# Four phases of a two-layer transformer kernel: engine loops written out as straight-line code

## The chip, the cores and the metric

One core of one Trainium2 chip runs the whole program. The metric is the device time of one execution in microseconds. Differences are judged against the median of several runs of the kernel before.

## The reference

Two layers work on x of shape 2 x 2048 x 256 (batch, token, channel). Each layer has an attention part and a feed-forward part, each behind a layer norm with a scale and shift from a small modulation product, and each added back with a gate.

```python
# layer 0
c_kv = h @ W_kv_down                      # 128 wide
k_rope, q_rope = rotary(c_kv @ W_k_rope), rotary(h @ W_q_rope)
k, v, q = heads(c_kv @ W_k_up), heads(c_kv @ W_v_up), heads(h @ W_q)
attn = softmax(causal((q k + q_rope k_rope) / scale)) v @ W_o
out  = top-2 experts of 8, three ReLU layers each
# layer 1
z   = softmax over tokens of (h @ W_A.T) / 4          # 16 heads
out[i] = sum over j <= i of z[i - j] * v[j]           # a Toeplitz product per head
out = out @ W_O.T + b_O
# last feed-forward: x_prev is x shifted by one token
r = sigmoid(mix_r(h, h_prev) @ W_r.T);  k = relu(mix_k(h, h_prev) @ W_k.T) ** 2
x = x + gate * r * (k @ W_v.T)
```

## The kernel before

The kernel is nine phases, one after the other, with a barrier between two phases: setup, project, attention, attn_out, route, experts, mix, mix_out, ffn. In each phase every engine has its own instruction stream, written by hand, and waits on semaphores. Nothing is scheduled by a planner.

Tokens go through the phases in chunks of 512 (`CH`), four chunks (`NCH`) for each of two batches (`NB`). A half-iteration is one chunk of one batch. Phases project, mix and ffn share the helper `one_ahead` (lines 236 to 244). It first starts the first half-iteration, then runs `work(it, 0, ...)` and `work(it, 1, ...)` for three values of `it` in an engine loop (`Fori`), and writes the fourth value out behind the loop. `work` also prepares the half-iteration that comes next. TensorE, VectorE and ScalarE each run this helper with their own `work`. In a loop, `it` is a register: addresses and semaphore values that depend on it are computed by small register instructions of that engine (FUSED_REGOPS, ALU_OP, MOVE), and the loop ends in a COMPARE_BRANCH.

What matters of the four stages:
- **project** (50 to 212 us). A half-iteration on TensorE is transposes of the normalised rows (L433), the products of `ckv`, `q`, rope, `k` (L467) and `v` (L486) into six PSUM banks. On VectorE it is the low halves of q (L358), the next layer norm (L72 to L81), two rope blocks (L364 to L373) and the low halves of k (L358). TensorE's `freed` makes it wait until VectorE has read a bank: the first product of `ckv` for batch 0 waits for the rope block of `kr` of the half before (L373), and `q0` of batch 1 does too. SyncE stores 11 pieces for each half (L327 to L336), in a loop of its own.
- **mix** (1817 to 1900 us): layer norm, transposes (L1633), z (L1641) and values (L1658), then a softmax over all tokens, written out.
- **Toeplitz products** (1900 to 2046 us, inside phase mix). For each head and batch SyncE loads a skewed copy of z of 1 MB into one of four buffers `tz` (L1560), TensorE makes 16 products with fp32 weights (L1673), and VectorE copies the result (L1598). Each of the three has a loop of eight iterations with four of these groups in its body.
- **ffn** (2112 to 2221 us). On TensorE a half-iteration is k products (L1905), the next transposes (L1895), r products (L1915) and v products (L1924). On VectorE it is the next normalise (L1823), the next mix (L1833, L1837) and the output (L1857, L1859). GpSimd squares k (L1798), SyncE stores (L1811), both in loops of four.

Attention (212 to 1225 us) has a loop too (`units`, L616; SyncE's at L729): one iteration is two units of one group of four heads and one batch. Its iteration is far longer than the others.

Of the kernel before, what the change touches and what calls it, by code (L numbers as in the profile page):

```python
# [21 lines left out]
NCH = T // CH  # L22
NT = T // P
NH, HD, DR, DC = 16, 16, 32, 128
# [211 lines left out]
def one_ahead(eng, start, work):  # L236


    start(0, 0)
    with eng.Fori(0, NCH - 1) as it:  # L240
        work(it, 0, (it, 1))
        work(it, 1, (it + 1, 0))
    work(NCH - 1, 0, (NCH - 1, 1))
    work(NCH - 1, 1, None)


def phase_project(nc, g):


    with ExitStack() as c:  # L250
# [62 lines left out]
        @block.sync  # L313
        def _(sp):
            for s in (*tr_done, *ht_ready, *stored, *ckv_ready, *rope_ready, *hi_ready, *lo_ready, *va_ready):
                sp.sem_inc(s, 1)
            for dst, src in ((wkv[:, :, :], g.i["wkv"].rearrange("(k p) n -> p k n", p=P)),
                             (wq[:, :, :], g.i["wq"].rearrange("(k p) n -> p k n", p=P)),
                             (wqr[:, :, :], g.i["wqr"].rearrange("(k p) n -> p k n", p=P)),
                             (wkr[:, :], g.i["wkr"]), (wku[:, :], g.i["wku"]), (wvu[:, :], g.i["wvu"])):  # L320
                sp.dma_start(dst, src).then_inc(w_ld, 16)
            sp.dma_start(cs[:, :], g.i["cs"]).then_inc(cs_ld, 16)
            with sp.Fori(0, NCH) as it:
                for b in range(NB):
                    cols = bass.ds(b * T + it * CH, CH)
                    sp.wait_ge(rope_ready[b], 2 * it + 3)
                    sp.dma_start(g.d_qrh[:, cols], roth[0:32, b, 0, :]).then_inc(stored[b], 16)  # L327
                    sp.dma_start(g.d_krh[:, cols], roth[0:32, b, 1, :]).then_inc(stored[b], 16)
                    sp.wait_ge(hi_ready[b], 4 * it + 5)
                    sp.wait_ge(lo_ready[b], 4 * it + 5)  # L330
                    for n, (dh, dl) in enumerate(((g.d_qh, g.d_ql), (g.d_kh, g.d_kl))):
                        for k in range(KT):
                            sp.dma_start(dh[k * P:(k + 1) * P, cols], hi[:, b, n, k, :]).then_inc(stored[b], 16)
                            sp.dma_start(dl[k * P:(k + 1) * P, cols], lo[:, b, n, k, :]).then_inc(stored[b], 16)
                    sp.wait_ge(va_ready[b], 2 * it + 3)
                    sp.dma_start(g.d_va[:, bass.ds(b * NT + it * TPC, TPC), :],  # L336
                                 va[:, b].rearrange("p t h d -> p t (h d)")).then_inc(stored[b], 16)
            for b in range(NB):
                sp.wait_ge(stored[b], 16 * NST * NCH + 1)
# [1160 lines left out]
def phase_mix(nc, g):  # L1500


    with ExitStack() as c:
# [37 lines left out]
        @block.sync  # L1541
        def _(sp):
            for s in (*mix_done[0], *mix_done[1], *tr_done, *ht_ready, *z_ready, *v_ready, *mix_read[0], *mix_read[1]):
                sp.sem_inc(s, 1)
            sp.dma_start(wa[:, :, :], g.i["wa"].rearrange("(k p) h -> p k h", p=P)).then_inc(w_ld, 16)
            sp.dma_start(wv[:, :, :], g.i["wv"].rearrange("(k p) n -> p k n", p=P)).then_inc(w_ld, 16)

            sp.wait_ge(zn_ready, 1 + NB)
            sp.dma_start(g.d_z[:, :, 0:P], zero[:, :, :]).then_inc(zstored, 16)
            sp.dma_start(g.d_z[:, :, P:], z[:, :, :]).then_inc(zstored, 16)  # L1550
            sp.wait_ge(zstored, 32)
            with sp.Fori(0, NH // 2) as it:
                for p in range(2):
                    for b in range(NB):
                        sp.wait_ge(mix_done[p][b], it + 1)


                        row = g.d_z[bass.ds(it * 2 + p, 1), b, 1:1 + T]
                        src = bass.AP(row.tensor, row.offset, [[1, P], [1, T]])
                        sp.dma_start(tz[:, p, b, :], src).then_inc(toep_ld[p][b], 16)  # L1560

        @block.vector
        def _(dve):
            ch = Chain(dve, chain_s)

            def normalise(it, b):
                ch.at((it * NB + b) * LN_LINKS)
                dve.wait_ge(tr_done[b], 2 * it + 1)
                ln_rows(dve, ch, g.x, b * NT + it * TPC, hn[:, b], ln, b, it).then_inc(hn_ready[b], 1)

            def work(it, b, ahead):
                if ahead:
                    normalise(*ahead)
                if not isinstance(it, int):
                    values(it, b)

            def values(it, b):
                for j in range(2):
                    dve.wait_ge(v_done[b], 2 * it + j + 1)
                    dve.tensor_copy(vn[:, bass.ds(b * NT + it * TPC + 2 * j, 2), :],  # L1580
                                    ps[:, 4 + 2 * b + j, :].rearrange("p (t c) -> p t c", t=2)).then_inc(v_ready[b], 1)
            one_ahead(dve, normalise, work)
            ch.at(NCH * NB * LN_LINKS)
            for b in range(NB):
                dve.wait_ge(z_ready[b], NCH + 1)
                ins = dve.tensor_reduce(nmax[:, b:b + 1], z[:, b, :], AX.X, ALU.max, negate=True)
                ins.then_inc(nmax_ready, 1)
            dve.wait_ge(exp_ready, NB)
            ch.link(dve.reciprocal(zrec[:, :], zsum[:, :]))
            for b in range(NB):  # L1590
                dve.tensor_scalar(z[:, b, :], z[:, b, :], zrec[:, b:b + 1], None, ALU.mult).then_inc(zn_ready, 1)
            for b in range(NB):
                values(NCH - 1, b)
            with dve.Fori(0, NH // 2) as it:
                for p in range(2):
                    for b in range(NB):
                        dve.wait_ge(mix_done[p][b], it + 2)
                        dve.tensor_copy(g.mixed[:, b * NT:(b + 1) * NT, bass.ds((it * 2 + p) * HD, HD)],  # L1598
                                        ps[:, 2 * p + b, 0:C].rearrange("p (t d) -> p t d", d=HD))\
                           .then_inc(mix_read[p][b], 1)  # L1600
# [26 lines left out]
        def _(pe):  # L1627
# [8 lines left out]
            def work(it, b, ahead):  # L1636
                pe.wait_ge(w_ld, 32)
                pe.wait_ge(ht_ready[b], 2 * it + 3)
                pe.wait_ge(z_ready[b], it + 1)
                for k in range(KT):  # L1640
                    ins = pe.matmul(ps[0:NH, 2 + b, :], wa[:, k, :], ht[:, b, k, :], start=(k == 0), stop=(k == KT - 1))  # L1641
                ins.then_inc(z_done[b], 1)
                if isinstance(it, int):

                    if ahead:
                        transposes(*ahead)
                else:
                    values(it, b, ahead)
# [15 lines left out]
            for b in range(NB):  # L1664
                pe.wait_ge(v_ready[b], 2 * NCH + 1)

            with pe.Fori(0, NH // 2) as it:
                for p in range(2):
                    for b in range(NB):
                        pe.wait_ge(toep_ld[p][b], (it + 1) * 16)  # L1670
                        pe.wait_ge(mix_read[p][b], it + 1)
                        for d in range(NT):
                            ins = pe.matmul(ps[:, 2 * p + b, d * HD:C], tz[:, p, b, d * P:(d + 1) * P],  # L1673
                                            vn[:, b * NT:(b + 1) * NT - d, bass.ds((it * 2 + p) * HD, HD)],
                                            start=(d == 0), stop=(d == NT - 1))
                        ins.then_inc(mix_done[p][b], 1)
# [76 lines left out]
def phase_ffn(nc, g):  # L1753

    with ExitStack() as c:
# [34 lines left out]
        @block.gpsimd  # L1790
        def _(pool):
            pool.memset(ht[:, :, :, CH:CH + 1], 0.0).then_inc(zero_done, 1)
            with pool.Fori(0, NCH) as it:
                for b in range(NB):
                    pool.wait_ge(v_done[b], 2 * it + 1)
                    for k in range(KT):
                        pool.wait_ge(kr_ready[b], 2 * it + k + 2)
                        pool.tensor_tensor(ka[:, b, k, :], kr[:, b, k, :], kr[:, b, k, :], ALU.mult)\  # L1798
                            .then_inc(ka_ready[b], 1)

        @block.sync
        def _(sp):
# [2 lines left out]
            sp.dma_start(wr[:, :, :], g.i["wr"].rearrange("(k p) n -> p k n", p=P)).then_inc(w_ld, 16)  # L1805
            sp.dma_start(wk[:, :, :], g.i["wk"].rearrange("(k p) n -> p k n", p=P)).then_inc(w_ld, 16)  # L1806
            sp.dma_start(mu[:, :, :], g.i["mu"]).then_inc(w_ld, 16)
            with sp.Fori(0, NCH) as it:
                for b in range(NB):
                    sp.wait_ge(y_ready[b], 2 * it + 3)  # L1810
                    sp.dma_start(g.out[bass.ds(b * T + it * CH, CH), :].rearrange("(t p) c -> p t c", p=P), y[:, b])\  # L1811
# [233 lines left out]
```

## Time and profile before

| | |
|---|---|
| median of 3 runs | 2202.44 us (2201.98 to 2204.1) |
| the profiled execution's own time | 2223.14 us |
| its span, first to last instruction | 2221.6 us |
| TensorE / VectorE / ScalarE / GpSimd busy | 77% / 55% / 39% / 13% |
| mean granted TensorE clock | 0.89 of full speed |

The profiled execution is 20.7 us longer than the median of the others, and 1.5 us of it lie outside the span. Stages are read from windows of the span. TensorE appears twice: PE is the matmul, PEld the load of its weights. A small q behind an engine's name marks its sequencer, which handles branches, register instructions and the issue of DMAs. These don't count as busy time.

### The profile page before, as it was taken

The page shows a single profiled execution, that of the slowest core. Times are in us where ns is not written, and L with a number is a line of the kernel's source. Part 1 is how long each engine was busy: PE and PEld are TensorE (multiplying, and loading weights), DVE is VectorE, ACT ScalarE, POOL GpSimd, SP SyncE. Part 2 cuts the span into 40 slices and gives each one's busy share as a digit, 9 for nine tenths or more (in the row PEclk, how much of TensorE's full clock was granted, in tenths as well). Part 3 has the DMA queues.
Part 4 walks back from the last instruction along what each step waited for, and adds up shares of the span by engine and source line. Part 5 has one row for each costly group of instructions (what it writes and reads, how often), then busy time and mean ns, then how long its engine had stood idle before and what let it go on. Part 6 is the DMA issues. An engine that isn't in the chain of part 4 may idle for free. (4 is left out here: it accounts for less than half of the span.)

```text
span 2221.6 us, 34675 instructions
## 1 busy us (share of the span) xinstructions
PE 1714.1 (77%) x12628; PEld 847.3 (38%) x12628; DVE 1214.5 (55%) x3101; ACT 860.1 (39%) x1137; POOL 287.6 (13%) x356
## 2 busy tenths in 40 slices
PE   4774278999999999999999264304888977999988
PEld 3332012333333333333333232102434454899556
DVE  4675577887877878697850134301444545101466
ACT  0231034566656666566667013202545513000133
POOL 1001283000000000000000110272212100000011
PEclk8898589999999999999999676656999969999989
DMA  5234941221203030303000310027666300774011
GB/s 177 93 117 147 164 137 62 57 40 49 49 26 72 25 72 22 65 25 73 25 25 36 113 61 0 32 107 159 131 141 144 100 5 0 234 235 140 1 38 47
DMA packets 88965, 180.41 MB, mean 81 GB/s; under 512 B 12529, under 2 KB 61330, under 8 KB 83538
## 3 DMA queue, kind: packets, MB, share of 16 engines
q1 hardware_dynamic: 69072, 109.73, 20.3%
q0 software_dynamic: 18656, 66.31, 8.8%
q8 instruction: 98, 1.61, 0.3%
q10 hardware_dynamic: 1090, 2.36, 0.3%
q14 instruction: 49, 0.40, 0.1%
HBM read 119.38 MB, written 57.85 MB: 80 GB/s over the span
## 5 line engine op out<-in xcount | busy, mean ns | idle before, releaser
L858 ACT ACTIVATE at_pr<-ps 128x1024 f32<-128x1024 f32 (+3 forms) x640 | 548.5, 894 | 361.9 <-PE ps L798 233.6
L892 DVE TENSOR_REDUCE at_mx<-ps 128x1 f32<-128x512 f32 x768 | 489.1, 685 | 173.2 <-PE ps L748 163.6
L795 PE MATMUL ps<-at_sq,at_sk 64*128 64x512 f16 (+3 forms) x2560 | 346.3, 349 | 22.7 <-DMA at_sq<-at_mr 18.7
L748 PE MATMUL ps<-at_sk,at_sq 64*128 64x512 f16 (+3 forms) x1280 | 236.8, 367 | 114.2 <-DMA at_vl<-d_va 43.3
L774 PE MATMUL ps<-at_pr,at_vl 128*32 128x512 f32 (+3 forms) x2560 | 300.7, 542 | 0.1
L889 DVE CUSTOM_DVE_ANT_0 at_seen<-ps,later 128x384 bf16<-128x384 f32 (+3 forms) x512 | 230.0, 488 | 5.4 <-issue 3.8
L798 PE MATMUL ps<-bq,bk 64*128 64x512 f16 (+3 forms) x1280 | 225.1, 348 | 0.0
L748 PEld LDWEIGHTS ps<-at_sk,at_sq 64*128 64x128 f16 x1280 | 62.1, 94 | 410.8 <-DVE at_mx L892 218.6
L795 PEld LDWEIGHTS ps<-at_sq,at_sk 64*128 64x128 f16 x2560 | 112.6, 95 | 129.2 <-ACT at_pr L858 35.7
L1673 PE MATMUL ps<-mi_vn,mi_tz 128*128 x1024 | 145.6, 305 | 2.2 <-DMA mi_tz<-d_z 2.2
L1673 PEld LDWEIGHTS ps<-mi_vn,mi_tz 128*128 128x128 f32 x1024 | 142.8, 192 | 5.3 <-issue 2.6
L665 POOL DMA_DIRECT2D d_o<-at_oc x32 | 17.3, 541 | 832.7 <-ACT at_oc L849 809.8
L1471 DVE CAST ex_hh<-ex_hf 128x1024 f16<-128x1024 f32 x46 | 32.1, 698 | 147.2 <-ACT ex_hf L1450 147.2
L1410 PE MATMUL ps<-ex_hh,ex_w 128*128 128x512 f16 x368 | 109.9, 380 | 0.8 <-DVE ex_hl L1473 0.8
L1410 PE MATMUL ps<-ex_xt,ex_w 128*128 128x512 f16 x276 | 76.3, 435 | 39.8 <-DMA ex_bias<-in_b 39.8
L1387 PE MATMUL ps<-ex_id,ex_xr 128*128 128x128 f16 x368 | 26.0, 227 | 100.5 <-DMA ex_xr<-d_rows 100.5
L1450 ACT ACTIVATE ex_hf<-ps,ex_bias 128x512 f32<-128x512 f32 x92 | 58.2, 683 | 105.1 <-PE ps L1410 105.1
L1437 ACT ACTIVATE ex_xt<-ps 128x2048 f16<-128x2048 f16 x23 | 43.2, 1877 | 121.9 <-PE ps L1387 121.9
L1598 DVE COPY mixed<-ps 128x256 f32 x32 | 13.6, 425 | 134.1 <-PE ps L1673 134.1
L1730 ACT ACTIVATE mo_at<-ps 128x512 f32<-128x512 f32 x16 | 8.7, 595 | 200.4 <-PE ps L1701 200.4
L798 PEld LDWEIGHTS ps<-bq,bk 64*128 64x128 f16 x1280 | 62.9, 95 | 59.8 <-issue 3.4
L774 PEld LDWEIGHTS ps<-at_pr,at_vl 128*32 128x32 f32 x2560 | 50.7, 108 | 78.6 <-issue 62.8
(239 smaller groups left out, 2091.8 us busy)
## 6 DMA issues: line engine op xcount, KB each, us to landing
mi_tz<-d_z SPq DMA_DIRECT2D x32, 1024.0 KB, 5.1
ex_w<-d_w POOLq DMA_DIRECT2D x23, 768.0 KB, 7.4
d_rows<-at_nil POOLq DMA_DIRECT2D x32, 379.5 KB, 3.0
ex_xr<-d_rows SPq DMA_DIRECT2D x23, 512.0 KB, 10.3
d_va<-pj_va SPq DMA_DIRECT2D x8, 1024.0 KB, 3.9
at_vl<-d_va SPq DMA_DIRECT2D x8, 1024.0 KB, 13.3
d_o<-at_oc POOLq DMA_DIRECT2D x32, 256.0 KB, 2.3
at_pw<-in_w POOLq DMA_DIRECT2D x24, 256.0 KB, 3.2
```

Source lines behind the costliest of these rows:

```text
L748: ins = pe.matmul(ps[:, MAXB + (slot + r) % RING, 0:hi_ - lo], sq[half[r], b, i, 0, qb * P:(qb + 1) * P], sk[half[r], b, i, 0, lo:hi_], st ...
L774: ins = pe.matmul(ps[32 * h:32 * h + 32, O, off:CH], vl[:, b, kb, 32 * h:32 * h + 32], pr[:, n % 2, h // 2, h % 2, off:CH], start=(kb == 0 ...
L795: pe.matmul(ps[:, 2 * f + r, off:CH], sk[half[r], b, f, part, k], sq[half[r], b, f, part, q], start=part == 0, stop=False)
L798: ins = pe.matmul(ps[:, 2 * f + r, off:CH], g.bk[half[r], b, k], g.bq[half[r], b, q], start=False, stop=t < 0)
L858: act.activation(pr[:, n % 2, f, :, off:CH], ps[:, 2 * f:2 * f + 2, off:CH], ACT.Exp, scale=INV_SCALE).then_inc(exp_done[f], 1)
L889: ins = dve.tensor_tensor_reduce(seen[:, turn, r, 0:n], src, g.later[:, CH - n:CH], 1.0, LOWEST, ALU.add, ALU.max, dst)
L892: ins = dve.tensor_reduce(dst, src, AX.X, ALU.max)
L1410: ins = pe.matmul(ps[:, 2 * PAIR[l, cc] + o, :], lhs, rhs, start=(i == 0), stop=(i == len(parts) - 1))
L1437: act.activation(xt[:, cc % 2], TURN, ACT.Copy).then_inc(xt_ready, 1)
L1450: ins = act.activation(hf[l][:, o, :], ps[:, 2 * PAIR[l, cc] + o, :], ACT.Relu, bias=bias[:, cc % BUF, l, o:o + 1])
L1471: dve.tensor_copy(hh[l][:, cc % 2], hf[l][:, :, :]).then_inc(high[l], 1)
L1673: ins = pe.matmul(ps[:, 2 * p + b, d * HD:C], tz[:, p, b, d * P:(d + 1) * P], vn[:, b * NT:(b + 1) * NT - d, bass.ds((it * 2 + p) * HD, HD ...
```

## The change

The loops of project, mix, Toeplitz products and ffn become Python loops, so every iteration is in the program with constant addresses and constant semaphore values. `one_ahead` serves project, mix and ffn on three engines. The two tests `isinstance(it, int)` told loop code from the written-out last chunk; they become tests on the number of the chunk and choose the same code as before. The order of the instructions on every engine, their tiles and the values that they wait for stay the same. Attention is not touched.

```diff
@@ one_ahead: project, mix and ffn, on TensorE, VectorE, ScalarE
     start(0, 0)
-    with eng.Fori(0, NCH - 1) as it:
+    for it in range(NCH):
         work(it, 0, (it, 1))
-        work(it, 1, (it + 1, 0))
-    work(NCH - 1, 0, (NCH - 1, 1))
-    work(NCH - 1, 1, None)
+        work(it, 1, (it + 1, 0) if it + 1 < NCH else None)
@@ phase_project, SyncE
-            with sp.Fori(0, NCH) as it:
+            for it in range(NCH):
@@ phase_mix, SyncE: the loads of tz
-            with sp.Fori(0, NH // 2) as it:
+            for it in range(NH // 2):
@@ phase_mix, VectorE
-                if not isinstance(it, int):
+                if it < NCH - 1:
                     values(it, b)
...
-            with dve.Fori(0, NH // 2) as it:
+            for it in range(NH // 2):
@@ phase_mix, TensorE
-                if isinstance(it, int):
+                if it == NCH - 1:
...
-            with pe.Fori(0, NH // 2) as it:
+            for it in range(NH // 2):
@@ phase_ffn, GpSimd
-            with pool.Fori(0, NCH) as it:
+            for it in range(NCH):
@@ phase_ffn, SyncE
-            with sp.Fori(0, NCH) as it:
+            for it in range(NCH):
```

## Rows read from the trace of the kernel before

**Rows 1.** The page: busy time and instructions of each engine; DMA queues: packets, MB, share of 16 engines.
```profile
PE 1714.1 (77%) x12628; PEld 847.3 (38%) x12628; DVE 1214.5 (55%) x3101; ACT 860.1 (39%) x1137; POOL 287.6 (13%) x356
...
q8 instruction: 98, 1.61, 0.3%
```

**Rows 2.** Busy time by stage: project, mix, Toeplitz products, ffn.
```profile
50.00:207.00 157.00, 110.37 (x304) 54.64 (x304) 106.76 (x238) 47.11 (x81) 7.93 (x3) 0.89 0.32 114
...
1817.00:1900.00 83.00, 59.78 (x224) 35.20 (x224) 43.56 (x133) 23.97 (x38) 0.00 (x0) 0.87 0.09 23
1900.00:2046.00 146.00, 145.64 (x1024) 142.79 (x1024) 13.29 (x32) 0.00 (x0) 0.00 (x0) 0.99 0.66 221
...
2112.00:2219.00 107.00, 94.09 (x384) 68.25 (x384) 72.12 (x130) 39.36 (x62) 17.12 (x17) 0.94 0.11 40
```

**Rows 3.** Timeline of VectorE in project: start, duration, line, operation, [idle before].
```profile
146.75 0.68 DVE L364 TENSOR_TENSOR pj_rc<-ps,pj_cs 64x512 f32<-64x512 f32 x1
...
154.13 1.29 DVE L358 TENSOR_TENSOR pj_lo<-ps,pj_hi 128x512 f16<-128x512 f32 x2
...
182.08 0.68 DVE L364 TENSOR_TENSOR pj_rc<-ps,pj_cs 64x512 f32<-64x512 f32 x1
...
189.28 1.29 DVE L358 TENSOR_TENSOR pj_lo<-ps,pj_hi 128x512 f16<-128x512 f32 x2
```

**Rows 4.** Timeline of TensorE in project, where batch 0 starts: last loop iteration, then written out.
```profile
133.78 3.78 PE L467 MATMUL ps<-pj_ht,pj_wkv 128*128 128x512 f32 x4 [4.47 <-DVE bk L373]
...
154.16 3.70 PE L467 MATMUL ps<-pj_ht,pj_wq 128*128 128x512 f32 x8 [1.71 <-DVE bk L373]
...
170.34 3.34 PE L467 MATMUL ps<-pj_ht,pj_wkv 128*128 128x512 f32 x4 [4.56 <-DVE bk L373]
```

**Rows 5.** Timeline of TensorE in mix: transposes of two neighbouring halves.
```profile
1844.76 1.09 PE L1633 MATMUL ps<-ident,mi_hn 128*128 128x128 f32 x8 [0.82 <-DVE mi_hn L81]
...
1852.25 1.09 PE L1633 MATMUL ps<-ident,mi_hn 128*128 128x128 f32 x8 [0.93 <-DVE mi_hn L81]
```

**Rows 6.** Timeline of TensorE in the Toeplitz products, all 32 groups.
```profile
1900.09 145.64 PE L1673 MATMUL ps<-mi_vn,mi_tz 128*128 x1024 [2.16 <-DMA mi_tz<-d_z]
```

**Rows 7.** Branches of TensorE's sequencer, from three lines: ns min/median/max.
```profile
L240 PEldq COMPARE_BRANCH  x9: 76/213/240, 91.3 to 2190.7; - x9
```
```profile
L1667 PEldq COMPARE_BRANCH  x8: 76/208/223, 1917.9 to 2043.8; - x8
```
```profile
L616 PEldq COMPARE_BRANCH  x3: 83/3964/4227, 657.9 to 1122.2; - x3
```

**Rows 8.** Timeline of TensorE between two attention units: within an iteration, across the branch.
```profile
546.21 0.61 PE L795 MATMUL ps<-at_sq,at_sk 64*128 64x512 f16 x4 [1.26 <-DMA at_sq<-at_mr]
```
```profile
662.12 1.04 PE L795 MATMUL ps<-at_sq,at_sk 64*128 64x512 f16 x4 [3.29 <-issue]
```

**Rows 9.** One attention unit without a branch inside: its busy times, TensorE's waits.
```profile
546.21:662.11 115.90, 107.39 (x1090) 37.72 (x1091) 91.50 (x262) 70.53 (x84) 4.32 (x8) 1.00 0.21 47
```
```profile
PE ps L748 <- DVE at_mx L892: 1.8, 7, 0.4
PE ps L748 <- DVE at_mx L889: 1.4, 4, 0.6
```

**Rows 10.** Timeline of TensorE in ffn: transposes in the loop, and written out (last row).
```profile
2139.26 1.09 PE L1895 MATMUL ps<-ident,ff_hn 128*128 128x128 f32 x8 [0.54 <-DVE ff_hn L1823]
...
2186.63 1.09 PE L1895 MATMUL ps<-ident,ff_hn 128*128 128x128 f32 x8 [0.38 <-DVE ff_hn L1823]
...
2198.30 1.10 PE L1895 MATMUL ps<-ident,ff_hn 128*128 128x128 f32 x8 [0.24 <-DVE ff_hn L1823]
```

**Rows 11.** Register instructions around copies and DMA issues: lines 1598, 1560, 1811.
```profile
L1598 DVEq FUSED_REGOPS  x32: 65/67/69, 1906.5 to 2045.8; - x32
```
```profile
L1560 SPq FUSED_REGOPS  x32: 43/49/61, 1894.1 to 2027.8; - x32
L1560 SPq MOVE mi_tz<-d_z x32: 29/29/29, 1894.2 to 2027.9; - x32
...
DMA to landing us min/median/max: 4.9/5.1/11.5
```
```profile
L1811 SPq FUSED_REGOPS  x8: 46/46/52, 2137.1 to 2218.2; - x8
```

## The prediction

> **What bounds the kernel now.** I started from the page, because it counts instructions: this change alters only which instructions the engines' sequencers handle and how code reaches them. TensorE runs 12628 matmuls and as many weight loads, and the queue named "instruction" moved 98 packets of 1.61 MB, 16 KB each [rows 1]. 25256 instructions over 98 packets are 258 for each, so nearly every instruction that TensorE executes was fetched about once. Next come the stages [rows 2]. The Toeplitz stage is TensorE at 145.64 of 146.00 us, at a granted clock of 0.99. In ffn TensorE is busy for 94.09 of 107 us. In project and mix neither TensorE (110.37 of 157, 59.78 of 83) nor VectorE (106.76, 43.56) fills the stage, so the two take turns. For each stage I then read the timeline of the two engines across three places: inside a loop iteration, across the branch, and in the last chunk, which the kernel before already writes out. This last one is the best evidence there is. It is the code after the change, measured in the trace of before. Comparing a half-iteration in the loop with the written-out one prices the change without any model of a register instruction.
>
> **The change part by part.** Removed are the branches, the register instructions, and what both delay. Added is code to be fetched. Nothing moves.
>
> *Project.* Here the path goes round: VectorE's rope blocks end, TensorE starts the next products at once (it stood 4.47 us for batch 0 and 1.71 us before `q0` for batch 1, both ended by VectorE L373 [rows 4]), ScalarE copies, and VectorE goes on. So what VectorE loses inside a rope block is on the path in every half. From the start of the first rope to the low halves of k the loop takes 154.13 - 146.75 = 7.38 us, the written-out half 189.28 - 182.08 = 7.20 us [rows 3]. The six loop halves lie between 7.38 and 7.41, the two written out at 7.20 and 7.21. That is 0.19 x 6 = 1.1 us saved. The layer norm ahead of it takes the same time in both, since its register instructions run while the copy before it is busy. One thing gets worse: in the loop TensorE stood 4.47 us where it waits for L373, in the written-out half 4.56 [rows 4], with the wait now in two instructions. 0.1 us for the two more starts of batch 0 is 0.2 us lost. The branch itself (213 ns on TensorE [rows 7]) lies within the 4.47 us in which TensorE waits anyway; without that cover it would cost 0.2 us for each of two. At the end of project SyncE issues nine DMAs one after the other and the phase ends when the last has landed. Each loses a MOVE, which I price by the 29 ns of the same instruction at L1560 [rows 11]: 0.25 us, between 0 (if the issue itself is what takes the time) and 0.5 with the gaps around it.
>
> *Mix.* TensorE's idle before the transposes alternates, 0.82 and 0.93 us [rows 5], between the two batches; the longer one has a register instruction of TensorE ahead of its wait. Three times 0.1 us: 0.3 us, between 0 and 0.3.
>
> *Toeplitz products.* All 32 groups are one unbroken stretch of TensorE [rows 6], and the eight branches of about 208 ns [rows 7] leave no gap in it: the sequencer reaches the first at 1917.9 us, and the four groups that it closes keep TensorE busy for almost 2 us longer. So seven back edges and 32 register instructions are worth 0. If that cover were gone, they would be 7 x 0.21 + 32 x 0.05 = 3 us. VectorE's copies are 0.43 us in a group of 145.64 / 32 = 4.55 us and wait for TensorE. What counts is the two ends. The first load of tz, for which TensorE stands 2.16 us [rows 6], has two register instructions and a MOVE ahead of its issue, 49 + 49 + 29 ns and a loop setup [rows 11]: 0.3 us with the gaps between. The last copy has 67 ns ahead of it [rows 11] and the next phase waits for it: 0.1 us.
>
> *Ffn.* TensorE goes round in 11.4 us of work plus one gap, the wait for the normalised rows. Over the five loop halves in steady state the gap is 0.54, 0.47, 0.38, 0.42 and 0.38 us, in the written-out half 0.24 [rows 10]. The sum of the differences is 0.99 us. It comes from VectorE, whose output (L1859) and normalise (L1823) wait for addresses in registers; ScalarE and GpSimd have slack. The last store of the kernel has 46 + 29 ns of register work ahead of it [rows 11]: 0.1 us.
>
> *The code.* By the counts of rows 2, the loop bodies repeat in TensorE's stream: project executes 608 instructions in four iterations, mix 448, ffn 768, of which two of the four repeat a body already in the program; of the 2048 in the Toeplitz stage seven eighths do. Written out, that is 304 + 224 + 384 + 1792 = 2704 more instructions to fetch, at 258 for each packet 10 to 11 more packets, seven of them in the Toeplitz stage. I price them at 0. The cover is the sequencer's lead: an attention unit streams 2181 matmuls and weight loads in 115.90 us, 53 ns for each, all of it code that comes in as it goes, and within it TensorE waits for VectorE alone, 3.2 us, and never for issue [rows 9]. The Toeplitz stage takes 145.64 us for 2048, 71 ns for each, so a packet of code lasts 18 us there. It does share the DMA engines with tz loads at a share of 0.66 [rows 2], but these have slack too: a buffer is wanted again after four groups, 18 us, and a load lands in 5.1 us [rows 11]. If the cover failed, a stop would cost what the attention branch costs, 3.29 - 1.26 = 2.0 us and more [rows 8].
>
> Sum: 1.1 - 0.2 + 0.25 + 0.3 + 0.3 + 0.1 + 1.0 + 0.1 = 2.95, so 3 us saved of the profiled execution's 2223.14 (span 2221.6): 2220.1 us. In the runs without a profile the same instructions run, so I subtract it from the median: 2202.4 - 3.0 = 2199.4 us, 0.14% less. That is inside the 0.2%, about 4.4 us, that a measurement of this kernel can tell from no change.
>
> **Rivals.**
>
> *1. The back edges hide a stall.* In attention the taken branch takes TensorE's sequencer 3964 and 4227 ns against 83 ns when it falls through [rows 7], and TensorE stands 3.29 us where it otherwise stands 1.26 [rows 8]. If the six taken branches of project, mix and ffn cost 2.0 us each, the gain would be 12 us more: 2187 us. Against it: those branches took 213 ns, at most 240 [rows 7]. What differs is the body, 152, 112 and 192 instructions (a quarter of the counts above) against some 4360 for two attention units [rows 9]. The Trainium skill (Runtime: NRT & Kernel Launch, "Instruction fetch mechanics") says that a taken branch whose target is outside the current window of two pages, 256 instructions each, has to fetch it from memory first, and that kernels prefer full unrolling for this. By that rule the seven back edges of the Toeplitz loop, whose body is 256 matmuls and weight loads plus waits, could stall too, and 7 x 2.0 us more would give 2185 us. For attention the trace agrees with it; in the Toeplitz loop it shows no gap [rows 6]. I give this rival 3%.
>
> *2. Fetching code stops TensorE, and the kernel gets slower.* The place is the Toeplitz stage, where TensorE has no idle time to lose and the DMA engines are two thirds busy. Each stop would cost at least 2.0 us, plus time at half clock after it. It turns the sign from the second stop on, and passes 0.2% from the fourth; all seven and the three others would be 10 x 2.0 - 3 = 17 us: 2219 us. Rows 9 speak against it: straight-line code at a faster rate did not stop. But there the DMA share was 0.21. 6%.
>
> *3. The layout of attention's code moves.* The 304 instructions that project gains shift the target of attention's back edge against the 16 KB packets. Two taken branches stop TensorE for 2.0 us more than a normal boundary. A target near the end of its packet needs a second fetch before TensorE can run on, another 2 us each with a slow clock behind it: up to 4 us lost, 2203.5 us, which is no change; with more it would be slower. A better layout could give back about as much: 2195.5 us. Project also has a stretch of half clock at each start of batch 0, whose length moves with small shifts, 1 us either way.
>
> *4. The saving is larger than the pairs show.* Register instructions may also delay the first halves of each phase, ScalarE's and GpSimd's waits, and nine DMA issues by 0.06 us each. With every bound at its high end (0.5 in project's tail, 3 us of uncovered branches in the Toeplitz stage) the sum is 6.2 us: 2196.2 us. Together with the good half of rival 3 this is the case "faster", 24%.
>
> **How the numbers follow.** The forecast and the harmless part of rival 3 stay within 0.2%: 66%. Faster by over 0.2%, below 2198.0: 3% from rival 1 and 21% from rivals 3 and 4. Slower, above 2206.8: 6% from rival 2, 4% from the bad end of rival 3. Range: down to 2194.5 for rivals 3 and 4 together, up to 2205.0 for the bad layout with 1.5 us of clock.
>
> **What would show it.** After the change: no register instruction and no branch of lines 240, 1552, 1594, 1667, 1793, 1808; 108 or 109 packets of 16 KB instead of 98, some eight of them in the Toeplitz stage instead of one; rope to low halves 7.20 us in all eight halves; gaps of 0.24 before all ffn transposes; Toeplitz stage unchanged at 145.6 us without a gap inside. The prediction is wrong if that stretch has gaps ended by issue, or if the stops at 662 and 894 us in attention change by more than 1 us.

## The result, and the profile after

The changed kernel takes 2196.16 us (median of 20 runs) where the kernel before takes 2202.21 us: a ratio of 0.9968, 95% interval [0.9957, 0.9978]. The medians are 6.05 us apart, about twice the 3 us that was forecast; the ratio, taken by itself, stands for 7.0 us, its interval for 4.8 to 9.5. The measured time is inside the range, but in the case "faster", which had 24%, and not in "no change", which had 66%.

The page after, its engine line and its queue for instructions (packets, MB, share of 16 engines):

```profile
PE 1710.3 (78%) x12628; PEld 848.0 (39%) x12628; DVE 1209.0 (55%) x3101; ACT 853.8 (39%) x1132; POOL 289.0 (13%) x356
...
q8 instruction: 107, 1.75, 0.3%
```

The work is the same as in [rows 1], with nine more packets of code. The profiled span is 2198.3 us against 2221.6 before, and that 23.3 us must not be read as the effect. I cut every profile at the first TensorE instruction of each phase. The experts' phase, which the change doesn't touch, takes 302.1 us in the profile of before and 288.0 in that of after. In the twelve profiles that follow it lies anywhere from 284 to 296 us, in kernels with loops and without. It is also shorter with the whole change than in the kernels of the same set that keep these loops, each time: 288.0 against 302.1, 285.0 to 285.7 against 292.3, 284.2 against 285.5 to 288.7. Whether that is chance or an effect of the change on code that it doesn't touch is not shown; if it is an effect, the stages below leave it out. Compared are the stages that the change touches, over all profiles that share the code in question. In us from one cut to the next ("mix" ends where the first Toeplitz product starts, so it holds the wait for the first load):

```
                     loops (mean, lowest to highest)   written out
project              182.0  180.4-183.5   8 profiles   181.2  180.5-182.4   6 profiles
mix                   79.2   78.8- 79.9   8             78.3   77.4- 79.2   6
Toeplitz products    146.5 in 7, 144.85 in 1           144.71 in all 6
ffn to the end       107.4  107.1-107.8   7            103.5-103.8 in 3, 105.0-105.2 in 4
```

The changed kernel's own profile has 104.97 in the last row. With it the stages give 0.8 + 0.9 + 1.8 + 2.4 = 5.9 us, and the medians 6.05. The agreement is closer than the interval of the times can support. The largest part is in ffn. TensorE there (start, duration, line, operation, [idle before]):

```profile
2101.60 6.49 PE L1903 MATMUL ps<-ff_xm,ff_wk 128*128 128x512 f32 x8 [6.30 <-issue]
...
2115.71 3.60 PE L1903 MATMUL ps<-ff_xm,ff_wk 128*128 128x512 f32 x8
...
2126.93 3.60 PE L1903 MATMUL ps<-ff_xm,ff_wk 128*128 128x512 f32 x8
...
2138.14 3.60 PE L1903 MATMUL ps<-ff_xm,ff_wk 128*128 128x512 f32 x8
2141.58 1.04 PE L1893 MATMUL ps<-ident,ff_hn 128*128 128x128 f32 x8
```

A round takes 11.22 us, and the transposes follow the k products with no idle time at all. Before, the rounds took 11.96, 11.90, 11.81, 11.85, 11.81 and, written out, 11.68 us; their gaps stand in [rows 10]. So even the written-out half of before, by which the prediction priced the change, was 0.46 us slower than any half is now. The reason shows on VectorE and GpSimd. First the kernel before at the same place, a loop half:

```profile
2183.78 0.69 DVE L1859 TENSOR_TENSOR ff_y<-ff_y,x 128x512 f32<-128x512 f32 x1 [0.17 <-DVE ff_y L1857]
2184.39 2.10 DVE L1823 TENSOR_SCALAR ff_hn<-x,mv_all,rs_all 128x256 f32 x4
```
```profile
2185.31 1.04 POOL L1798 TENSOR_TENSOR ff_ka<-ff_kr 128x512 f32<-128x512 f32 x1 [9.16 <-ACT ff_kr L1879]
```

and the kernel after:

```profile
2139.17 0.69 DVE L1857 TENSOR_TENSOR ff_y<-ff_y,x 128x512 f32<-128x512 f32 x1
2139.78 1.38 DVE L1821 TENSOR_SCALAR ff_hn<-x,mv_all,rs_all 128x256 f32<-128x256 f32 x4
```
```profile
2140.80 1.25 POOL L1796 TENSOR_TENSOR ff_ka<-ff_kr 128x512 f32<-128x512 f32 x1 [8.52 <-ACT ff_kr L1877]
```

Four normalises took 2.10 us and now take 1.38. GpSimd's square beside them took 1.04 and now takes 1.25. In this half VectorE was idle for 0.17 us ahead of the addition before them, and no longer is. Line by line (ns, least / median / most):

```profile
L1823 DVE TENSOR_SCALAR ff_hn<-x,mv_all,rs_all x32: 405/408/1209, 2112.6 to 2197.0; 128x256 f32 x24, 128x256 f32<-128x256 f32 x8
```
```profile
L1821 DVE TENSOR_SCALAR ff_hn<-x,mv_all,rs_all x32: 403/406/413, 2091.9 to 2174.4; 128x256 f32<-128x256 f32 x32
```

In the kernel before, the fourth normalise of each of the last six halves takes 1.13 to 1.21 us, and it starts between 210 ns after GpSimd's square and 22 ns ahead of it. After the change it starts 42 to 53 ns ahead, takes 0.40, and the square takes 1.25 to 1.26. So one of the two goes at full speed and the other stands. Which one is a matter of the start, but not exactly of who is first, since 22 ns ahead VectorE still lost. A blocked normalise always ends 0.15 us after the square does. The Trainium skill (SBUF — State Buffer, "SBUF: two separate sides") says that GpSimd shares a port pair with a VectorE instruction that runs in a two-port mode or has two inputs in SBUF (the latter only against a GpSimd instruction that reads SBUF). It calls the pair an exclusive lock, held for the whole instruction by the one that starts first. The trace agrees for VectorE, which loses 0.7 to 0.8 us and ends with the square. As loser GpSimd takes only 0.21 us more, less than the 0.36 for which the normalise still runs. No run shows in which mode the normalise runs.

With ffn written out VectorE wins every time. The idle time of 0.17 us that is gone points to its register instructions as what made it late. But the written-out half of before, which has none of them on VectorE, lost too, and GpSimd's loop is written out by the same change. So which engine's register work tips the order is argued and not shown.

The Toeplitz products after, and their first 7 us before and after (stretch, its length, busy time of PE, PEld, DVE, ACT, POOL, then the granted clock, DMA share, GB/s):

```profile
1881.21 143.93 PE L1671 MATMUL ps<-mi_vn,mi_tz 128*128 128x256 f32 x1024 [1.64 <-DMA mi_tz<-d_z]
```
```profile
1900.09:1907.00 6.91, 6.91 (x35) 6.46 (x36) 0.05 (x1) 0.00 (x0) 0.00 (x0) 0.75 0.96 407
```
```profile
1881.21:1888.00 6.79, 6.79 (x45) 6.64 (x46) 0.42 (x1) 0.00 (x0) 0.00 (x0) 1.00 1.03 403
```

The difference lies in the first group of 32 products: 6.19 us before, with 3.4 us of it at 1.2 GHz right after TensorE had waited 2.16 us for the first load, and 4.48 us after a wait of 1.64. All later groups take 4.49 us in both kernels (the last, with its end, 4.64), with no gap. The queue for code in the same stage:

```profile
q8 instruction: 8, 0.13, 0.3%
```

Eight packets, as predicted, and none of them is seen by TensorE. Project, VectorE and then TensorE (beside [rows 3] and [rows 4]):

```profile
146.38 0.68 DVE L362 TENSOR_TENSOR pj_rc<-ps,pj_cs 64x512 f32<-64x512 f32 x1
...
153.58 1.29 DVE L356 TENSOR_TENSOR pj_lo<-ps,pj_hi 128x512 f16<-128x512 f32 x2
```
```profile
134.33 3.65 PE L465 MATMUL ps<-pj_ht,pj_wkv 128*128 128x512 f32 x4 [4.36 <-DVE bk L371]
...
153.60 3.70 PE L465 MATMUL ps<-pj_ht,pj_wq 128*128 128x512 f32 x8 [1.55 <-DVE bk L371]
```

The rope part is 7.20 us, as predicted; the waits of 4.47 and 1.71 us became 4.36 and 1.55. The first and the last of the nine DMA issues at the end of project, before and after:

```profile
203.50 0.35 SPq L333 DMA_DIRECT2D d_qh<-pj_hi  x1
...
207.60 0.33 SPq L336 DMA_DIRECT2D d_va<-pj_va  x1
```
```profile
204.13 0.36 SPq L331 DMA_DIRECT2D d_qh<-pj_hi  x1
...
207.95 0.45 SPq L334 DMA_DIRECT2D d_va<-pj_va  x1
```

The last start follows the first after 4.10 us before and 3.82 after. Mix (beside [rows 5]), two neighbouring halves:

```profile
1826.08 1.09 PE L1631 MATMUL ps<-ident,mi_hn 128*128 128x128 f32 x8 [0.73 <-DVE mi_hn L81]
1833.38 1.09 PE L1631 MATMUL ps<-ident,mi_hn 128*128 128x128 f32 x8 [0.73 <-DVE mi_hn L81]
```

Both batches now wait 0.73 us, less than the better of the two did before, and the round is 7.30 us instead of 7.49 and 7.38.

### The profile page after: what moved, and what is told of

Same layout as the page of the kernel before. It is cut to its first block and busy times, and to the rows that moved or that the text cites. A ratio compares the mean times of both kernels' runs of the same rounds, so it can differ in the third digit from the quotient of the medians.

```text
span 2198.3 us, 33784 instructions
## 1 busy us (share of the span) xinstructions
PE 1710.3 (78%) x12628; PEld 848.0 (39%) x12628; DVE 1209.0 (55%) x3101; ACT 853.8 (39%) x1132; POOL 289.0 (13%) x356
## 5 line engine op out<-in xcount | busy, mean ns | idle before, releaser
L1671 PE MATMUL ps<-mi_vn,mi_tz 128*128 128x256 f32 (+15 forms) x1024 | 143.9, 303 | 1.6 <-DMA mi_tz<-d_z 1.6
L1596 DVE COPY mixed<-ps 128x256 f32<-128x256 f32 x32 | 13.6, 425 | 131.7 <-PE ps L1671 131.7
```

## The experiments

**1. The parts alone.** In each of three kernels one part is written out, and the fourth is the kernel before unchanged. This is the edit in the ffn one, cut short: the first change is made for GpSimd and for SyncE, the second for VectorE, ScalarE and TensorE. `one_ahead_flat` is the same pipeline over a Python `range`. The other kernels do it in project, and in mix with the Toeplitz products.

```diff
-            with pool.Fori(0, NCH) as it:
+            for it in range(NCH):
...
-            with sp.Fori(0, NCH) as it:
+            for it in range(NCH):
...
-            one_ahead(dve, start, work)
+            one_ahead_flat(dve, start, work)
...
-            one_ahead(act, modulated, work)
+            one_ahead_flat(act, modulated, work)
...
-            one_ahead(pe, transposes, work)
+            one_ahead_flat(pe, transposes, work)
```

> The kernel before once more, unchanged. It gives a second profile of before and says how far two timings of one kernel lie apart. Ratio 1.000 within 0.15%. If the unchanged stages explain the 23 us between the two profiled executions, the experts stage (302 us from the first row gather to the first transpose of mix in the first profile of before, 288 us in the one after) will come out near 288 us here too. In ffn, GpSimd's first square of each half starts just before VectorE's fourth normalise and that one takes about 1.1 us in seven of seven halves.

> Only ffn written out (all five engines). Theory A (port order): without the register instruction ahead of L1859 VectorE's fourth normalise starts before GpSimd's square instead of after it, takes 0.41 us, and TensorE's round falls from 11.8 to 11.2 us: 3.5 us saved, ratio 0.9984. Theory B (my sum, register instructions alone): 1.1 us, ratio 0.9995. Theory C (layout of attention's code and luck of the clock): no change in ffn's rounds.

> Only project written out. My sum gives 1.1 us, ratio 0.9995, with the half-iterations at 7.2 us of rope. Theory C (attention's back edges stop TensorE for less, since its code is shifted by the 304 instructions that project gained): attention from its first matmul to its last is 2 to 4.5 us shorter than in the kernels that leave project's loop, ratio 0.9975 to 0.9985.

> Only mix and the Toeplitz products written out. My sum gives 0.7 us, ratio 0.9997: mix 0.3 us for TensorE's idle before the transposes at 0.73 to 0.82 us everywhere, Toeplitz groups at 4.49 us as before, first load 0.3 us earlier. Rival: a stretch of half clock at the first Toeplitz group that was in before and not after is tied to the change; then it is gone here too and the stage is 1.7 us shorter. If it is chance, it may come or go.

Measured, ratio to the kernel before: unchanged 1.0001 [0.9986, 1.0015]; ffn 0.9959 [0.9943, 0.9975]; project 0.9994 [0.9984, 1.0005]; mix and Toeplitz 0.9976 [0.9965, 0.9987]. Ffn is the largest part and project the smallest. The three savings add up to 0.7%, where the whole change gave 0.3%, and ffn's 0.4% is 9 us where its stage shows 4.0. So these times rank the parts but don't measure them; the stages do that better. The profile of ffn alone has the blocked normalise gone (406 to 415 ns) and rounds of 11.21 to 11.22; that of mix has the Toeplitz stage at 144.71.

The project kernel gives an answer that was not asked for. Its Toeplitz products are still in the loop, and TensorE waits 2.60 us for the first load, yet the stage takes 144.85 us, because no half clock falls on it:

```profile
1887.17:1894.00 6.83, 6.83 (x45) 6.68 (x46) 0.42 (x1) 0.00 (x0) 0.00 (x0) 1.00 1.05 404
```

So the loop itself costs at most 0.14 us there, and the 1.7 us that the stage otherwise gains is the clock of the first group.

**2. The whole change again, and two attempts to turn the race around.** The first repeats the whole change. The second is the kernel before with GpSimd's first square meant to be late (six waits on a count already reached), the third the changed kernel with VectorE's last addition meant to be late (two such waits).

```diff
                         if k == 0:
+                            for _ in range(6):
+                                pool.wait_ge(v_done[b], 2 * it + 1)
```

> The whole change once more, on the chip of this group. Ratio 0.997 as before. By stages, against the profiles that keep the stage's loops: ffn 3.7 us shorter in its rounds, mix 1.2, project to the start of attention 1.9, Toeplitz stage 0 or 1.7 us shorter (by whether its first group falls in a stretch of half clock). If the experts stage was chance in the first pair of profiles, it takes about 295 us here too.

> The kernel before with all its loops; GpSimd alone passes six waits that are already met ahead of its first square of each ffn half, about 0.3 us. Nothing is removed. Theory A (port order): VectorE's fourth normalise now starts first, takes 0.41 us instead of 1.13, and TensorE's rounds fall to 11.2 us: 3.7 us saved, ratio 0.9983. Theory B (register instructions cost what they delay, no more): rounds stay at 11.8, ratio 1.000, or slower if the square was on the path.

> The whole change, with two waits that are already met put ahead of each addition of the ffn output on VectorE (L1859), some 0.13 us where the loop had a register instruction. Theory A: the fourth normalise starts after GpSimd's square again and is blocked for 0.7 us; rounds go back from 11.2 to 11.7 or 11.8 and the kernel loses 3.5 to 4.2 us against the whole change. Theory B: it loses 0.13 us in each of seven halves at most, 0.9 us, and nothing at all if VectorE has slack by then.

Measured: 0.9973 [0.9959, 0.9987], 1.0007 [0.9994, 1.002] and 0.9987 [0.9972, 1.0003]. The last two say nothing of the race. GpSimd and VectorE started within some 15 ns of where they do without the waits, so both expectations were left untested. What the third does tell is how far two builds with the same timing lie apart: 0.9973 and 0.9987, which is within their intervals.

**3. The attention loop written out as well**, which the change left alone: here with the whole change, and in the next set by itself.

```diff
-            with eng.Fori(0, NG - 1) as grp:
+            for grp in range(NG - 1):
...
-            with sp.Fori(0, NG - 1) as grp:
+            for grp in range(NG - 1):
```

> The whole change, and attention's loops written out as well. The two taken branches stop TensorE for 2.9 to 3.6 us each where a normal boundary has 1.26, and a stretch of half clock follows: each unit with a stop in it takes about 115.7 us against 113.8 to 114.3 without. Theory of the missed target: both stops go, units at 113.8 to 114.2 us, 7 to 8 us less than the whole change, ratio to before 0.9935. Rival: the rest of the two units is lost somewhere else in the loop code (register instructions on VectorE, 40 ns x 900), and the gain is larger; or code is then fetched too late in the longer program and TensorE stops for it, in which case nothing is gained.

Measured: 2186.51 us, 0.9911 [0.989, 0.9933], the lowest median of the study. Attention takes 1002.15 us instead of some 1014, and 998.73 in the kernel with attention alone (below). That is more than the 7 to 8 us of the two stops; the expectation's rival, that the loop code loses time elsewhere too, came true.

**4. The race with instructions that take time.** In the kernel before, GpSimd does a one-element product and three one-element memsets ahead of the first square of each half. In the changed kernel, VectorE does two one-element memsets ahead of the second addition.

```diff
+                        if k == 0:
+                            pool.tensor_tensor(pgap[:, 0:1], kr[0:1, b, 0, 0:1], kr[0:1, b, 0, 0:1], ALU.mult)
+                            for n in range(1, 4):
+                                pool.memset(pgap[:, n:n + 1], 0.0)
```

> The kernel before with all its loops; GpSimd alone does four one-element operations ahead of its first square of each ffn half (one product, three memsets), 0.2 to 0.4 us. Nothing is removed, work is added. Theory A (port order): the fourth normalise now starts before the square, takes about 0.41 us instead of 1.13 (or 0.5 behind a one-element operation), and TensorE's rounds fall from 11.8 to 11.2 or 11.3 us: 3.5 us less in the ffn stage, 104 us instead of 107.5. Theory B (register instructions cost what they delay): rounds of 11.8 us, stage of 107.5 us. The ratio is 0.9984 by A and 1.000 by B, near the noise of it, so the stage decides.

> The whole change, with two one-element memsets ahead of each addition of the ffn output on VectorE, 0.1 to 0.2 us each time, about what the loop's register instruction took. Theory A: the fourth normalise falls behind the start of the square again, is blocked until it ends, and TensorE's rounds go back from 11.2 to 11.7 or 11.8: 3.5 to 4 us more in the ffn stage. Theory B: 0.2 us a round at most, 1.4 us.

> The kernel before with attention alone written out, and every other loop kept. From the run that wrote out both: attention's units at 112.55 us instead of 114.2 to 116.2, 12 to 13 us less, ratio 0.994. If that gain needed the others' code to be straight too (one layout of the code), it will be smaller than 10 us.

> Only ffn written out, as in an earlier run whose ratio was 0.9959 [0.9943, 0.9975], where its stages give 0.9983. If stages decide, the ratio comes out between 0.997 and 0.9995 here, and rounds at 11.2 us again. If ffn's loops cost something that the stages don't show, 0.996 again.

*GpSimd late* measured 0.9997 [0.9979, 1.0016]. Not all rounds became fast, as my theory had it; two of six did. The four normalises of the first four of them:

```profile
2119.03 2.35 DVE L1828 TENSOR_SCALAR ff_hn<-x,mv_all,rs_all 128x256 f32 x4
...
2131.17 2.35 DVE L1828 TENSOR_SCALAR ff_hn<-x,mv_all,rs_all 128x256 f32 x4
...
2143.23 1.38 DVE L1828 TENSOR_SCALAR ff_hn<-x,mv_all,rs_all 128x256 f32 x4
...
2154.61 2.13 DVE L1828 TENSOR_SCALAR ff_hn<-x,mv_all,rs_all 128x256 f32 x4
```

and TensorE's rounds in the same kernel, from one start to the next:

```profile
2117.14 3.60 PE L1910 MATMUL ps<-ff_xm,ff_wk 128*128 128x512 f32 x8
...
2129.35 3.60 PE L1910 MATMUL ps<-ff_xm,ff_wk 128*128 128x512 f32 x8
...
2141.49 3.60 PE L1910 MATMUL ps<-ff_xm,ff_wk 128*128 128x512 f32 x8
...
2152.71 3.60 PE L1910 MATMUL ps<-ff_xm,ff_wk 128*128 128x512 f32 x8
...
2164.70 3.60 PE L1910 MATMUL ps<-ff_xm,ff_wk 128*128 128x512 f32 x8
```

The fourth normalises of the six rounds take 1381, 1380, 408, 1153, 406 and 1380 ns, and the rounds 12.21, 12.14, 11.22, 11.99, 11.21 and 11.97 us. It is one kernel with every register instruction of the loop in place. Where VectorE is not blocked, the round is as short as written out; where it is, the round is longer by 0.75 to 1.0 us. So in ffn the register instructions act through the race, and add nothing seen where it is won. TensorE's back edge of 207 ns, at 2148.9 us, lies in the first of the two free rounds. The small operations failed as a delay because they seem to take part in it. A blocked normalise is now 1.38 us instead of 1.13. In the two free rounds GpSimd's one-element product starts 54 and 57 ns ahead of the normalise, in the others at least 99 ns ahead.

*VectorE late* measured 0.9985 [0.9968, 1.0003]. The memsets take time, but the normalise still starts 30 to 36 ns ahead of the square, so the order never turned and no round was lost:

```profile
L1868 DVE MEMSET ff_vgap<- x32: 59/59/59, 2108.6 to 2187.5; 1x1 f32 x32
```
```profile
L1831 DVE TENSOR_SCALAR ff_hn<-x,mv_all,rs_all x32: 399/402/411, 2084.9 to 2167.6; 128x256 f32<-128x256 f32 x32
```

As a test of the loss it is inconclusive. It does show where the race is decided: 30 ns ahead VectorE is free here, and 20 to 25 ns ahead it was blocked (the written-out half of before, in the six other profiles with ffn loops).

*Ffn again* measured 0.9982 [0.9965, 0.9999], the first time 0.9959. This is what its stages give, as one side of the expectation had it. In both profiles the six rounds are 11.21 to 11.22 and ffn takes 103.5 and 103.8 us, 3.6 to 3.9 less than the mean with loops.

*Attention alone* measured 2188.67 us, 0.9925 [0.9898, 0.9951], so its gain does not need the other changes. Its second unit:

```profile
541.24:653.78 112.54, 106.86 (x1091) 37.26 (x1092) 89.76 (x262) 70.23 (x84) 4.30 (x8) 1.00 0.21 48
```

Each unit in the middle takes 112.5 us, against 115.90 in [rows 9]. TensorE's waits over some four units, 540 to 1000 us, first before and then with attention written out (us in total, times, longest):

```profile
PE ps L748 <- DVE at_mx L889: 6.7, 20, 0.6
PE ps L748 <- DVE at_mx L892: 6.6, 27, 0.4
PE ps L795 <- DMA at_sq<-at_mr: 6.1, 3, 3.6
PE ps L795 <- issue: 3.3, 1, 3.3
```
```profile
PE ps L748 <- DVE at_mx L892: 6.3, 24, 0.4
PE ps L795 <- DMA at_sq<-at_mr: 5.8, 5, 1.2
PE ps L748 <- DVE at_mx L889: 5.1, 21, 0.4
```

The two stops of 3.3 and 3.6 us at the back edge are gone, and with them the half clock behind each. That gives 7 to 8 us. Units without a stop also shrank, from 114.2 to 112.5 us. It fits that VectorE's register instructions no longer make its maxima late, but the waits for the maxima fell by only 1.9 us over four units, of some 6.7 us that four such units shrank. No run takes these apart from the rest of the loop, so this second half stays open.

## Why the prediction was right or wrong

**The mechanism was right for less than half of the saving.** The 0.8 us of project and the 0.9 of mix are register work that left paths of waits, as the sum had it. The 2.4 us of ffn come from a race between two engines, which the change tipped, and the 1.8 of the Toeplitz products from TensorE's clock. The sum had neither, so that the time still fell inside the range is partly luck.

Most of the signs came out. Branches and register instructions of the six lines are gone, and so is the SyncE loop of project (L323), which the list had left out. 15 of the 20 branches left are attention's, and the five others stand alone outside any loop. 107 packets of code were moved, where 108 or 109 were expected, eight of them in the Toeplitz stage. They cost nothing, as priced. Rope to low halves is 7.20 us. Two signs did not: the gaps before the ffn transposes are 0 and not 0.24 us, and TensorE's Toeplitz stretch is 143.93 us and not 145.6.

The row for the cover of code, [rows 9], was misread. The unit from 546.21 to 662.11 us is not one without a branch: it holds the back edge at 657.9 and TensorE's stop of 3.29 us, ended by issue. The unit before it, from 432.00 to 546.21, has neither and takes 114.21. So a normal unit streams code slightly faster than was said, and the argument holds.

The size was off by a factor of two, in these terms:

- **Ffn, 1.0 us.** This is the term that failed: the six rounds got shorter by 3.7 us, and 2.4 net in this profile. The step "the written-out half is the code after the change, measured in the trace of before" assumed that this half was free of the cost. It was not: there the fourth normalise took 1.21 us, the longest of all. A look at the durations of line 1823 (405 / 408 / 1209) would have shown it. The term counted only the spread among blocked halves. Removing the gap also gave more than its 0.24 us: 11.68 against 11.22 is 0.46. Of the 3.7 us about 1.2 is given back in this kernel. 1.0 of that is the half clock at the start of ffn, which reaches further into the first k products: 6.49 us for the eight (first row of ffn above) where the kernel with only ffn written out has this:

```profile
2102.64 5.46 PE L1912 MATMUL ps<-ff_xm,ff_wk 128*128 128x512 f32 x8 [6.11 <-issue]
```

- **Toeplitz, 0 for the loops, 0.3 and 0.1 at the ends.** The loops are right (at most 0.14 us). So is the first load: it is issued at most 0.03 us after the store of z has landed, where the loop took 0.36. The stage gained 1.8 us because the first group now runs at full clock, a term that the sum didn't have. TensorE's wait for the first load was 2.0 to 2.35 us in the seven profiles with half clock there and is 1.0 to 1.8 in all six written-out ones, in part because TensorE's own products before it end later. That the shorter wait brings the clock is likely, but the project kernel had a longer wait and full clock, so it stays open.
- **Mix, 0.3 us.** Measured 0.9, in a row that also holds the 0.3 of the first load. The idle time became 0.73 for both batches where I had expected 0.82: again the "good" half of the pair was not free of the cost.
- **Project, 1.1 - 0.2 + 0.25 us.** Measured 0.8, with a scatter of 1 us from half clock at the starts of batch 0, and the part alone gave 0.9994. The two extra waits cost nothing (4.36 us, not 4.56). The nine DMA issues gained what was forecast. Each lost its MOVE and became longer, 0.43 to 0.46 us instead of 0.33 to 0.40 for most, but from one start to the next they now take 0.48 us instead of 0.51. The last transfer lands 7.85 to 7.89 us after VectorE's last low half in the six kernels with project written out, and 8.10 to 8.13 after it in the eight others: 0.24 us, against 0.25 in the sum.

**The rivals.** *Back edges that hide a stall*: fell for these loops; the round that holds TensorE's back edge and wasn't blocked took 11.22 us, as written out (experiment 4). For attention's loop the cost is real and now measured. *Code fetch that stops TensorE*: fell, since the Toeplitz stage with eight packets has no gap and is at its fastest. *The layout of attention's code*: with this change the stops at 658 and 890 us are 3.09 and 2.93 us instead of 3.29 and 3.55, and attention takes 1012.5 to 1014.7 us over profiles with project written out and 1013.5 to 1015.9 over the other loops (1017.2 in the first). An effect of up to 1.4 us is neither shown nor excluded; 4 us is. *A larger saving than the pairs show*: this is what happened, and to the size, 2196.2. That was luck: its stated reasons (uncovered branches, more from project's tail) were not the cause; the race and the clock were.

## What to carry to other kernels

A written-out copy inside the old kernel is a good price for a change only if it has none of the cost itself: compare the durations of the same instruction over all its uses before the gaps. Where VectorE and GpSimd work at the same time, look at which of the two starts first. A few tens of ns decide there over 0.7 us. A loop with few iterations and a big body is worth writing out first: the small loops of this change were worth 6 us in all, and attention's 13 to 16 by the times (11 to 16 by its stage).

## What was not expected of the hardware

- A blocked engine shows in the trace as a longer instruction and not as a wait: 1.13 to 1.21 us for a normalise of 0.40.
- One-element operations seem to take part in the race too: 0.25 to 0.4 us of them on GpSimd made the blocked normalise longer, by 0.25 us in three rounds of four.
- The experts' phase took 284 to 302 us over all profiles, and 7 us more in one kernel than in another of the same later set, with the same code. The same ffn edit gave 0.9959 and 0.9982, at the edge of what the two intervals allow, and the whole change 0.9968 and 0.9973. The ffn stage, cut out of the profile, repeated to 0.3 us for the same edit.
